# A cross-attention transformer kernel: value matmuls of two key tiles issued back to back in the first attention

## The reference

```python
q = split_heads(x @ Wq)          # 8 heads of 64, x is (2048, 256) after a layer norm
k = split_heads(context @ Wk)    # context is (1601, 256)
v = split_heads(context @ Wv)
sim = jnp.einsum('bhid,bhjd->bhij', q, k) * scale
attn = jax.nn.softmax(sim, axis=-1)
out = jnp.einsum('bhij,bhjd->bhid', attn, v)
return out.transpose(0, 2, 1, 3).reshape(x.shape[0], x.shape[1], INNER) @ Wo + bo
```

## Time and profile before

| | us |
|---|---|
| median of 3 runs | 3039.99 |
| lowest, highest | 3038.23, 3055.99 |
| the profiled execution | 3034.52 |
| its span (first to last instruction) | 3032.7 |
| PE busy, share of the span | 2679.6, 88% |
| DVE busy | 1921.4, 63% |
| ACT busy | 1295.3, 43% |

### The profile page before, as it was taken

How to read it: one execution, slowest core, us unless ns; L and a number is a source line. 1 busy time by engine, 2 the same in 40 slices (tenths; PEclk the granted TensorE clock), 3 DMA queues, 4 the chain that set the end, 5 groups by cost and what they waited for, 6 DMA issues and landing times.

```text
span 3032.7 us, 33880 instructions
## 1 busy us (share of the span) xinstructions
PE 2679.6 (88%) x11824; PEld 1211.9 (40%) x11824; DVE 1921.4 (63%) x4953; ACT 1295.3 (43%) x1748; POOL 277.0 (9%) x220
## 2 busy tenths in 40 slices
PE   8999989998868875999979997749899999999978
PEld 3333333333422222555645555714233333333267
DVE  4777797788568755241642344734776777777576
ACT  3333333434445421112532223522655566666663
POOL 1000000000022219000025400000000000000011
PEclk9999999999979987999889998876998999999989
DMA  3000000000020014000022100071002003000032
GB/s 115 1 8 1 1 1 1 1 1 1 11 112 1 1 49 134 21 1 1 1 72 86 55 1 7 1 111 30 16 1 29 10 1 38 1 29 1 1 133 90
DMA packets 45879, 88.75 MB, mean 29 GB/s; under 512 B 5766, under 2 KB 33930, under 8 KB 44682
## 3 DMA queue, kind: packets, MB, share of 16 engines
q1 hardware_dynamic: 45706, 86.57, 10.5%
HBM read 78.79 MB, written 7.77 MB: 29 GB/s over the span
## 4 chain that ended last, share of the span: by engine, by line
PE 67%; DVE 19%; issue 7%; ACT 5%; DMA 2%; SPq 0%; DVEq 0%; POOL 0%; ACTq 0%; POOLq 0%
PE PS L2135 7%; PE PS L1258 6%; PE PS L1241 6%; PE PS L2090 6%; PE PS L2116 5%; DVE pm L701 4%; PE PS L892 4%; PE PS L591 3%; PE PS L541 3%; DVE acc L723 3%; DVE R L728 2%; PE PS L1219 2%; PE PS L577 1%; PE PS L874 1%; PE PS L2158 1%
## 5 line engine op out<-in xcount | busy, mean ns | idle before, releaser
L2278 DVE CUSTOM_DVE_ANT_0 trash<-PS,mb 128x400 bf16<-128x400 f32 (+1 forms) x1024 | 529.7, 574 | 188.5 <-PE PS L2090 187.0
L2219 ACT ACTIVATE P<-PS 128x1024 f32<-128x1024 f32 (+1 forms) x416 | 410.2, 1021 | 245.1 <-PE PS L2116 241.2
L2090 PE MATMUL PS<-Ks,Qs 96*128 96x400 bf16 (+1 forms) x1024 | 341.5, 347 | 48.7 <-DMA Ks<-k_parts 33.8
L663 ACT ACTIVATE P<-PS 128x1024 f32<-128x1024 f32 (+1 forms) x208 | 212.4, 1023 | 286.1 <-PE PS L578 283.4
L2116 PE MATMUL PS<-Qs,Ks 99*128 99x512 bf16 (+1 forms) x832 | 309.2, 386 | 11.9 <-ACT Qs L2205 11.6
L701 DVE TENSOR_REDUCE pm<-PS 128x1 f32<-128x400 f32 (+1 forms) x512 | 269.8, 560 | 60.7 <-PE PS L553 59.8
L2135 PE MATMUL PS<-P,V 128*17 128x512 f32 (+1 forms) x1664 | 256.7, 605 | 2.0 <-ACT P L2219 2.0
L2090 PEld LDWEIGHTS PS<-Ks,Qs 96*128 96x128 bf16 x1024 | 96.6, 98 | 343.5 <-DVE pm L2278 235.4
L591 PE MATMUL PS<-P,V 128*64 128x512 f32 (+1 forms) x832 | 226.6, 623 | 6.2 <-ACT P L663 6.2
L723 DVE TENSOR_TENSOR acc<-acc,P 128x1024 f32<-128x1024 f32 (+1 forms) x176 | 212.9, 1210 | 3.1 <-ACT P L663 1.2
L553 PE MATMUL PS<-K,Q 128*128 128x400 bf16 (+1 forms) x512 | 167.2, 349 | 27.8 <-DVE pm L701 24.5
(11 more groups left out here) (329 smaller groups left out, 4404.1 us busy)
## 6 DMA issues: line engine op xcount, KB each, us to landing
mi<-in_mask SPq DMA_DIRECT2D x32, 800.5 KB, 4.4
We<-in_L_ffn_w SPq DMA_DIRECT2D x16, 1024.0 KB, 6.8
Wg<-gate_rows SPq DMA_DIRECT2D x8, 1024.0 KB, 11.6
Qs<-q_parts SPq DMA_DIRECT2D x24, 256.0 KB, 16.0
Ks<-k_parts SPq DMA_DIRECT2D x24, 200.1 KB, 17.7
q_parts<-T SPq DMA_DIRECT2D x8, 384.0 KB, 2.5
X<-in_x SPq DMA_DIRECT2D x4, 512.0 KB, 8.3
ex<-in_L_ffn_experts SPq DMA_DIRECT2D x8, 256.0 KB, 5.3
```

The lines of the kernel that those rows point to most:

```text
L663: e.activation(self.P[0:r, n % 4, :, :], PS[0:r, b:b + 2, :], ACT.Exp, scale=0.125).then_inc(*k.ac_exp.up(("A", n)))
L2090: e.matmul(PS[:, b, 0:kn], self.Qs[0:96, s, h, q0:q0 + 128], self.Ks[0:96, s, h, k0:k0 + kn], start=True, stop=True).then_inc(*k.pe_max.up ...
L2219: e.activation(self.P[0:r, n % 4, :, :], PS[0:r, b:b + 2, :], ACT.Exp, scale=0.25).then_inc(*k.ac_exp.up((3, n)))
L2278: e.tensor_tensor_reduce(k.trash[:, n % 2, 0:kn], PS[:, ring.of(("max", key)), 0:kn], self.mask.mb[:, t, k0:k0 + kn], 1.0, -3.0e38, ALU.ad ...
```

## The change

The value step no longer follows each tile's scores. In tiles 2, 4, ... 12 the value steps of the two tiles before are issued together after the scores; in odd tiles there is none; the last tile's value step of a block, with `take`, follows the scores of tile 0 of the next block, as before. The first of a pair thus comes one tile later than it did. Nothing else of the program is edited: slots, buffers, waits and instructions are the same, and since DVE walks the same list, its row-sum adds move with the value steps.

```diff
-        before = None
         for u in range(16):
             p, qb = u // 4, u % 4
             parts = []
@@
                 out.append((self, "score", (u, kt, 1)))
                 out += slots[4 * kt - 1] if kt else []
-                if before:
-                    out.append((self, "attend", before))
-                    if before[1] == KT - 1:
-                        out.append((self, "take", before[:1]))
-                before = (u, kt)
+                if kt == 0 and u:
+                    out += [(self, "attend", (u - 1, KT - 1)), (self, "take", (u - 1,))]
+                if kt and kt % 2 == 0:
+                    out += [(self, "attend", (u, kt - 2)), (self, "attend", (u, kt - 1))]
                 out += slots[4 * kt]
                 out += slots[4 * kt + 1]
-        out += [(self, "attend", before), (self, "take", before[:1])]
+        out += [(self, "attend", (15, KT - 1)), (self, "take", (15,))]
         return [s for s in out if s]
```

## The result

| | before | after |
|---|---|---|
| median, us | 3035.3 (17 runs) | 3060.3 (17 runs) |
| lowest, highest | 3026.3, 3061.6 | 3049.5, 3083.9 |
| span of the profiled execution | 3032.7 | 3057.9 |

The ratio of after to before is 1.0086, with a 95% interval of 1.0065 to 1.0106: 26 us slower, inside one per cent. Of all the runs of this case one was slow, an execution of the kernel `mixed` at 3211 us; its ratio leaves it out.

What follows compares the result with a forecast made beforehand. PE and DVE, both near full, were taken as coupled through three PSUM banks. Ring +9 (PE's 23 us saving spent there) and clock +9 made +18 us: 3052.5 profiled, 3058 as median; range 3022 to 3088.

Steps and rivals of the forecast that it cites:

- The saving: On PE in the first attention, joined value steps save 0.24 us a pair, 96 pairs, 23 us.
- The small loss that was left out: Denominator and value step 0, adjacent before in some blocks, no longer touch: 5 x 0.14 = 0.7 us back, not counted.
- The walk: Two blocks stepped through by trace spacings: 2.2 us lost with projections (453.9 to 502.8), 0.7 gained without (597.9 to 636.8).
- the ring's cost: PE held by the three PSUM banks that DVE frees: +9 us over all blocks, with PE's 23 us spent.
- The four blocks without projections: Blocks 3, 7, 11 and 12, where DVE binds already: 4 x -0.7 = -2.8 us.
- the three with four projections: Blocks 2, 6 and 10, taken between the two walked cases: 3 x 0.8 = 2.4 us lost.
- blocks 0 and 13 to 15: Blocks 0, 13 and 14 taken as nil; block 15, without maxima, keeps its saving: -1.4 us.
- PE's wait on L701 at 50 us or more: PE's wait for DVE's maximum reduction, 100 to 690 us, rises from 24 to 50 us or more.
- The clock: New PE holes at tile 5 lower the granted clock: nine falls at 1.0 us, 9 us (bounds 0 and 18).
- the saving arrives whole: Rival 1: PE sets the pace, adds hide under the longer value pair; 3040 - 23 = 3017 us, chance 0.13.
- Stalls without clock falls: Rival 2: PE waits in the ring but the granted clock does not fall; 3049 us, chance 0.2.
- The reason that I gave for the loss: At tile 5, PE lacks value step 4, its work while DVE is late; 2.2 us lost per block with six projections.

Runs made afterwards that it cites:

- mixed: A follow-up kernel; the study does not say under this name what it changed. One execution took 3211 us and is left out of its ratio.
- the kernel with the filler: Changed kernel plus six unused 512-column matmuls after the scores of tile 5 in each block; ratio to before 1.0028, stage 736.4 us.
- the shifted order: Changed kernel with pairs one tile later (3-4 at tile 5, 11-12 in the next block), adds moving along; ratio to before 1.0205, stage 796.6 us.

## Why the prediction was right, and where it was off

**The saving.** 0.24 us a pair by the earlier trace rows: the pair of 1.87 us is there to the hundredth. With PE's waits for maxima out of the way 17.9 of the 23 us arrive, spread otherwise than 1.4 us a block: about 2 in the blocks with projections, 0.3 in those without, and none over the last three together. The small loss that was left out, where denominator and value step 0 no longer touch, is 0.24 a time by the same working and not 0.14, 1.2 us in all.

**The walk.** For block 8 it had two scores and two maxima, then waits of 1.4 and 0.9 us at tile 5; measured 1.24 and 0.74. It took 2.25 us for two adds; they take 2.45. It put the ring's cost in the whole stage at +9; with the clock kept up it is 11.5 at most. In the kernel with the filler the blocks 1, 4, 5, 8 and 9 are 1.2, 1.9, 2.4, 3.0 and 2.4 us longer, a mean of 2.2, the number predicted for them. The other terms were off. The four blocks without projections were forecast 2.8 us shorter together and are 0.15 longer there; the three with four projections were forecast 2.4 longer and are 2.7 shorter; blocks 0 and 13 to 15 were forecast 1.4 shorter and are 3.2 longer. That the sum still comes near +9 is luck: these errors cancelled. The sign "PE's wait on L701 at 50 us or more" was just missed, with 46.

**The clock.** Nine falls were forecast before 690 us, ten came, each behind tile 5. Mis-sized was the price: 1.0 us each, 9 in all; measured 15.6. In all four blocks without projections the slowed stretch lasted twice as long as the one in the earlier trace rows, from 245 to 252 for one; against the kernel with the filler, blocks 3, 7, 11 and 12 are 2.4 to 3.2 us longer, the six others with a fall 1.1 to 1.5.

**The number.** 3058 was named and 3060.3 measured, but the forecast's step was +18 us and the real one 26. The rest came from the base: the three runs that were shown had a median of 3040.0, seventeen have 3035.3. So the number was off by 2 us and the step by 8: that the number came so near is luck.

**The rivals.** That the saving arrives whole fell with the first waits: it needed DVE in its adds under 0.4 us after PE enters a pair, and in block 8 DVE enters them 1.59 us after (480.55 and 482.14). *Stalls without clock falls* is what the filler kernel has before 690 us: +0.28%. The reason that I gave for the loss was half of it: I named the missing value step on PE and saw, but did not price, that the add of tile 2 had filled DVE's own wait for the projection's copy. The kernel with only the adds paired shows that half of the edit to be the dearer one.

## What to carry to other kernels

Before two short steps are joined to save the gap between them, look at what each of them covers: here both the value step on PE and the add on DVE stood where the other engine was late, and 0.24 us saved stood against up to 1.1 us of lost cover, one value step. Price the idle time that a reorder makes on TensorE twice, once as waiting and once as slowed matmuls after it; a few matmuls of no use in the hole tell the two apart. The second price is a chance and not a certainty: the same hole was followed by a fall in one block and not in another. Here it paid to join only in the blocks that had gained, and to leave the second engine's steps where they were.

## What the runs showed that I had not expected

The clock fell behind holes each of which was short: behind 1.24 and 0.74 us with a maximum of 0.34 between them at 485 us, and behind 1.06 and 0.98 us with the turn between them in the shifted order. It also stayed up behind 1.35 and 0.74 us at 345 us.

Paired adds under single value steps cost 55 us of the stage; with the value steps joined too it is 27. One half of an edit can cost twice what the whole does.
